# Output projection of two weight parts in one wide product, a second add per batch, and gaps in the order of work closed

## The chip, the cores and the metric

One core of one Trainium2 chip runs the whole program. The metric is the device time in microseconds (us), the median of several executions.

## The reference, cut to what matters

`x` is (32, 112, 256), `ctx_512` is (32, 375, 128), everything in float32.

```
x = x + tanh(g_xattn) * attention(layernorm(x), ctx, Wq, Wk, Wv, Wo, bo)     # 16 heads of 64
x = x + tanh(g_ffn)   * ffn(layernorm(x))
attention:  softmax(q k^T / 8) v, per head, then @ Wo + bo
ffn:        gates = softmax(xf @ router_w); top 2 of 14 experts, weights normalised
            sum of the 2 routed experts, plus 2 shared experts
            expert(x) = silu(rmsnorm(x) * rw @ W1) @ W2                      # 256 -> 512 -> 256
```

## The kernel before, in words

Every float32 product is made from two parts of each operand, `hi` (rounded to the fast matmul type) and `lo` (the rest): hi·hi, lo·hi and hi·lo are summed in PSUM. The function `three` (L584 to L588) issues these three matmuls, on the lines L586, L587 and L588.

**Attention** (`attend`). The weights are fused first: per head Wq Wk^T becomes `wqk`, and Wv Wo becomes `wvo` of 128 x 256, in the buffers `wvo_hi` and `wvo_lo`. Batches go in 16 pairs; of a pair, the 2 x 16 x 112 rows of scores make 28 steps of 128 rows. In a step, TensorE (PE) makes the scores of one tile (`scores`, 376 columns), a side job now and then (queries of two heads, the transposed context, the transposed x), the transposes of an earlier tile's probabilities (`turn`, L647), the weighted sums of the context (`sums`, 448 columns, a quad of four heads), and the output projection of single heads (`project`, 256 columns, into the left half of the bank `O`). VectorE (DVE) makes maxima (L872), reciprocals (L878), half of the scalings (L881) and all `lo` parts (L855); ScalarE (ACT) makes the exponentials (L763), the other scalings (L768) and all `hi` parts. GpSimd (POOL) splits the context, adds the bias, makes the Newton steps of the norms, and splits one routed expert's weights per pair (`split_expert`).

When the 16 heads of a batch are projected, DVE adds the bank `O` and the residual into `x2` (`ln2_add`, L911 to L916) and signals `x2_ready`. PE waits for `x2_ready` before the first head of the next batch (L671), because that head overwrites `O`. For the first batch of a pair the add falls into step 26; for the second it falls into step 12 of the next pair, just as the first projection of the next batch does.

PE, DVE and POOL run the first and the last pair as straight code, and pairs 1 to 14 in a hardware loop (`body_over_pairs`, L381; POOL L567); SP (the DMA issuer) loops over pairs 1 to 13 (L470); ACT is straight code.

**Start.** SP issues the loads in order: the two gates (L74, L75), x, Wk, Wq in two halves, and so on. PE first transposes Wk and Wq (L131, 24 transposes), then fuses.

**End of the attention.** In the last pair POOL makes `ln2_root(2p-1)`, `add_bias(p, 1)`, then scales the shared experts' weights (`scale_shared`, L1141) and splits them (`split_shared`, L1151). After the last step PE drains: it interleaves the first transposes of the normed rows (`sb["turn"]`, L1206) with the last sums and projections.

**Router, shared experts of groups 0 to 4** (`front`): 10 items of hidden (L1037, 512 columns) and output (L1045, 256 columns). The last item's output is preceded by the transposes of the first routed tile.

**Routed experts** (`routed_experts`): 69 tiles of 128 rows, each with hidden (L1702), transposes of the next rows (L1689), transposes of the hidden (L1712) and output: here `W2`'s hi and lo already lie side by side, so that output is one matmul of 512 columns (L1722) and one of 256 (L1726) per hidden block, and the two halves of the bank are added afterwards.

**Shared experts of groups 5 and 6** (`shared_after`), the sum, and the stores of `out` by SP (L1835), the last one of 512 KB.

## Time and profile before

| what | value |
|---|---|
| median of 3 runs | 1460.05 us (1459.97 to 1460.82) |
| the profiled execution's own time | 1458.97 us |
| its span, first to last instruction | 1457.2 us |
| mean granted TensorE clock | 0.999 |
| PE busy | 1435.2 us, 98% of the span, 9774 matmuls |
| PEld (weight loads, beside PE) | 1346.5 us, 92% |
| DVE busy | 1081.7 us, 74% |
| ACT busy | 935.1 us, 64% |
| POOL busy | 463.4 us, 32% |
| chain that ended last | PE 95%, DVE 2%, ACT 1%, issue 1% |

The busy share is an average over stages. A matmul's duration in the profile is its latency: the next one starts before it ends, so what a matmul costs is read from the distance of starts. "Idle before" names what ended the wait.

### The profile page before, as it was taken

What the parts mean: (1) busy time and instruction counts of PE and PEld (TensorE: products, weight loads), DVE (VectorE), ACT (ScalarE), POOL (GpSimd) and SP (SyncE); (2) the same over time, 40 slices, a digit from 0 to 9 for tenths busy, and PEclk for the clock granted to TensorE, in tenths of its full rate; (3) what the DMA queues carried; (4) which work ended last, traced back from release to release, by engine and by line L of the source; (5) the groups of instructions that cost most, each with busy time, mean ns of one, the idle gap of its engine ahead of it and who ended that gap; (6) DMA issues with size and microseconds to landing.
All of it is one profiled execution on the core that took longest, in us unless ns stands there. A gap on an engine that the chain in (4) does not pass through costs nothing.

```text
span 1457.2 us, 31992 instructions
## 1 busy us (share of the span) xinstructions
PE 1435.2 (98%) x9774; PEld 1346.5 (92%) x9774; DVE 1081.7 (74%) x2614; ACT 935.1 (64%) x2398; POOL 463.4 (32%) x688
## 2 busy tenths in 40 slices
PE   7999999999999999999999999999999999999998
PEld 7999999999999999999999999998789978888888
DVE  4878888888888888888788888878587444444448
ACT  6777777777776777777777777776453345455452
POOL 4313142231323413143231332417100145555520
PEclk9999999999999999999999999999999999999999
DMA  4010311213112131211303112150022346662235
GB/s 125 7 51 17 115 74 51 95 31 114 76 49 79 50 108 38 93 74 55 107 15 116 74 49 85 44 191 32 28 102 116 142 168 237 213 236 85 78 130 213
DMA packets 55583, 137.07 MB, mean 94 GB/s; under 512 B 10496, under 2 KB 38160, under 8 KB 51920
## 3 DMA queue, kind: packets, MB, share of 16 engines
q1 hardware_dynamic: 48880, 118.01, 23.4%
q0 software_dynamic: 6624, 18.13, 3.9%
q8 instruction: 35, 0.57, 0.2%
q14 instruction: 44, 0.36, 0.1%
HBM read 86.69 MB, written 49.43 MB: 93 GB/s over the span
## 4 chain that ended last, share of the span: by engine, by line
PE 95%; DVE 2%; ACT 1%; issue 1%; DMA 0%; SPq 0%; ACTq 0%; DVEq 0%
PE bank L586 19%; PE bank L587 18%; PE bank L588 18%; PE bank L647 10%; PE bank L1702 7%; PE bank L1045 6%; PE bank L1037 5%; PE bank L1722 4%; PE bank L1726 2%; PE bank L1712 2%; PE bank L1689 1%; PE bank L1218 1%; PE bank L602 1%; DVE pT_lo L855 1%; DVE nmax L872 0%
## 5 line engine op out<-in xcount | busy, mean ns | idle before, releaser
L763 ACT ACTIVATE prob<-bank,nmax 128x375 f32<-128x375 f32 x448 | 258.8, 578 | 190.3 <-DVE nmax L872 188.3
L855 DVE TENSOR_TENSOR pT_lo<-bank,pT_hi 125x384 fp32r<-125x384 f32 x448 | 246.2, 550 | 25.3 <-ACT pT_hi L774 23.7
L872 DVE TENSOR_REDUCE nmax<-bank 128x1 f32<-128x375 f32 x448 | 241.3, 539 | 29.9 <-PE bank L588 28.6
L647 PE MATMUL bank<-keep_ident,prob 128*125 128x128 f32 x1344 | 221.0, 273 | 0.9 <-DVE prob L881 0.9
L774 ACT CAST pT_hi<-bank 125x384 fp32r<-125x384 f32 x448 | 212.6, 475 | 1.7 <-PE bank L647 1.7
L647 PEld LDWEIGHTS bank<-keep_ident,prob 128*125 128x125 f32 x1344 | 201.4, 187 | 6.9 <-DVE prob L881 1.2
L586 PE MATMUL bank<-attend_wvo_hi,zT_hi 128*112 128x256 f32 x512 | 169.4, 331 | 0.7 <-DVE x L916 0.7
L586 PE MATMUL bank<-pT_hi,kv_hi 125*128 125x448 f32 x384 | 152.8, 398 | 4.3 <-DVE zT_lo L855 1.6
L586 PE MATMUL bank<-attend_kvT_hi,qp_hi 128*128 128x376 f32 x448 | 152.0, 339 | 1.4 <-ACT prob L763 1.3
L587 PE MATMUL bank<-attend_kvT_hi,qp_lo 128*128 128x376 f32 x448 | 149.8, 334 | 0.0
L588 PE MATMUL bank<-attend_kvT_lo,qp_hi 128*128 128x376 f32 x448 | 149.0, 333 | 0.0
L587 PE MATMUL bank<-attend_wvo_hi,zT_lo 128*112 128x256 f32 x512 | 144.2, 282 | 0.0
L855 DVE TENSOR_TENSOR qp_lo<-bank,qp_hi 128x448 fp32r<-128x448 f32 x128 | 79.7, 623 | 86.8 <-ACT qp_hi L756 85.0
L588 PE MATMUL bank<-attend_wvo_lo,zT_hi 128*112 128x256 f32 x512 | 143.7, 281 | 0.0
L518 POOL TENSOR_SCALAR rs<-mv 112x1 f32<-112x1 f32 x32 | 7.1, 221 | 422.7 <-DVE mv L925 422.6
L587 PE MATMUL bank<-xnT_hi,attend_wqk_lo 128*128 128x224 f32 x512 | 140.7, 275 | 0.0
L587 PE MATMUL bank<-pT_hi,kv_lo 125*128 125x448 f32 x384 | 140.7, 366 | 0.0
L588 PE MATMUL bank<-pT_lo,kv_hi 125*128 125x448 f32 x384 | 140.6, 366 | 0.0
L588 PE MATMUL bank<-xnT_lo,attend_wqk_hi 128*128 128x224 f32 x512 | 140.3, 274 | 0.0
L586 PE MATMUL bank<-xnT_hi,attend_wqk_hi 128*128 128x224 f32 x512 | 139.7, 273 | 0.6 <-DVE attend_wqk_lo L206 0.3
L768 ACT ACTIVATE prob<-prob,prob_inv 128x375 f32<-128x375 f32 x224 | 136.8, 611 | 1.4 <-DVE prob_inv L878 1.4
L881 DVE TENSOR_SCALAR prob<-prob,prob_inv 128x375 f32<-128x375 f32 x224 | 114.2, 510 | 8.0
(238 smaller groups left out, 3724.8 us busy)
## 6 DMA issues: line engine op xcount, KB each, us to landing
w_split<-we_split SPq DMA_DIRECT2D x14, 2048.0 KB, 6.9
keep_weights<-w_split SPq DMA_DIRECT2D x14, 2048.0 KB
we_in<-in_w SPq DMA_DIRECT2D x28, 512.0 KB, 5.9
keep_y_all<-y_rows SPq DMA_DIRECT2D x14, 512.0 KB, 9.1
kv_in<-in_ctx SPq DMA_DIRECT2D x32, 187.5 KB
h_rows<-hrow SPq DMA_DIRECT2D x32, 112.4 KB, 2.3
keep_h_in<-h_rows SPq DMA_DIRECT2D x7, 514.0 KB, 9.3
x_in<-in_x SPq DMA_DIRECT2D x16, 224.0 KB, 2.8
```

What stands on the lines that cost most here:

```text
L586: nc.tensor.matmul(out, a[0], b_[0], start=start, stop=False)
L587: nc.tensor.matmul(out, a[1], b_[0], start=False, stop=False)
L588: return nc.tensor.matmul(out, a[0], b_[1], start=False, stop=stop)
L647: last = nc.tensor.transpose(turn_bank_of(s)[0:MP, c * P:(c + 1) * P], prob[:, s % NB, c * MP:(c + 1) * MP], ident[:])
L763: nc.scalar.activation(prob[:, s % NB, :], score_bank(s)[:, 0:M], ACT.Exp, bias=nmax[:, s % NB:s % NB + 1], accum_out=psum_[:, s % NB:s % ...
L768: nc.scalar.mul(prob[:, s % NB, :], prob[:, s % NB, :], pinv[:, s % NB:s % NB + 1]).then_inc(norm_act, 1)
L774: nc.scalar.copy(pT["hi"][:, :, ring_place(s)], turn_bank_of(s)[0:MP, 0:MC * P].rearrange("p (c n) -> p c n", c=MC)).then_inc(pT_hi, 1)
L855: return nc.vector.tensor_tensor(dst, src, hi.bitcast(F32), ALU.subtract)
L872: nc.vector.tensor_reduce(nmax[:, s % NB:s % NB + 1], score_bank(s)[:, 0:M], AX, ALU.max, negate=True).then_inc(max_ready, 1)
L881: nc.vector.tensor_scalar(prob[:, s % NB, :], prob[:, s % NB, :], pinv[:, s % NB:s % NB + 1], None, ALU.mult).then_inc(norm_dve, 1)
L1045: last = nc.tensor.matmul(bank[:, (t % 2) * D:(t % 2 + 1) * D], hid[h][:, e, j, t * P:(t + 1) * P], sb["w2s_" + w][:, e, j, :], start=e == ...
L1702: last = nc.tensor.matmul(H_BANK[b][:, :], hT[a][:, b, k, :], part(slot, 2 * k * HID + at, HID), start=k == 0 and q == 0, stop=k == 1 and ...
```

## The change

- The two parts of the output weights lie side by side in one buffer `wvo` of [128, heads, 2, 256]; `wvo_hi` and `wvo_lo` become views of it. Per head, `project` issues one matmul of 512 columns (stationary zT_hi, moving hi and lo) and one of 256 columns (stationary zT_lo, moving hi) instead of three of 256. The hi·lo term then lies in the right half of `O`.
- `ln2_add` makes two adds, the second waits for the first, and `x2_ready` comes with the second.
- The loops over pairs of PE, DVE, POOL and SP are unrolled.
- The two gate loads are issued by ACT instead of SP. PE runs 20 transposes of the identity into an unused bank before it waits for Wk.
- POOL makes `scale_shared` ahead of `ln2_root(2p-1)` and of `add_bias(p, 1)`. `sb["turn"](pe, 1)` goes one step earlier in PE's drain.
- The first three tiles' rows are turned, and the first two routed hiddens made, between the parts of the last shared output. The routed stage's `T_BANK` and `O_BANK` are exchanged.
- The last store is cut into two of 256 KB.

```diff
-        def sync_gates(sp):
-            sp.dma_start(gates[:, 0:1], io["g_xattn"].partition_broadcast(P)).then_inc(gate_in, 16)
+        def sync_gates(act):
+            act.dma_start(gates[:, 0:1], io["g_xattn"].partition_broadcast(P)).then_inc(gate_in, 16)
...
+        def warm(pe):
+            pe.wait_ge(ident_ok, 1)
+            for _ in range(20):
+                nc.tensor.transpose(banks[7][:, 0:P], sb["ident"][:], sb["ident"][:])
...
         def body_over_pairs(eng, body):
-            body(0, FULL)
-            with eng.Fori(1, PAIRS - 1) as p:
-                body(p, FULL)
-            body(PAIRS - 1, LAST)
+            for p in range(PAIRS):
+                body(p, LAST if p == PAIRS - 1 else FULL)
...
             split_context(p, 1)
+            sb["scale_shared"](pool)
             ln2_root(2 * p - 1)
             add_bias(p, 1)
-            sb["scale_shared"](pool)
...
-                last = three(O[0:N, 0:D], [zT[q][:, qd % 2, j * N:(j + 1) * N] for q in ("hi", "lo")],
-                             [sb["wvo_" + q][:, h, :] for q in ("hi", "lo")], h == 0, h == H - 1)
+                hi, lo = (zT[q][:, qd % 2, j * N:(j + 1) * N] for q in ("hi", "lo"))
+                nc.tensor.matmul(O[0:N, :], hi, sb["wvo"][:, h, :, :].rearrange("p q d -> p (q d)"), start=h == 0,
+                                 stop=h == H - 1, skip_group_check=True)
+                last = nc.tensor.matmul(O[0:N, 0:D], lo, sb["wvo_hi"][:, h, :], start=False, stop=h == H - 1,
+                                        skip_group_check=True)
...
-            for s in range(last_tile(7) + 4, last_tile(7) + 6):
-                behind(last, s, (), True)
+            behind(last, last_tile(7) + 4, (), True)
             sb["turn"](pe, 1)
-            for s in range(last_tile(7) + 6, last_tile(7) + 9):
+            for s in range(last_tile(7) + 5, last_tile(7) + 9):
...
-                nc.vector.tensor_tensor(x2[:, b, :], O[0:N, 0:D], x_res[:, b, :], ALU.add).then_inc(x2_ready, 1)
+                nc.vector.tensor_tensor(x2[:, b, :], O[0:N, 0:D], x_res[:, b, :], ALU.add).then_inc(x2_half, 1)
+                dve.wait_ge(x2_half, bi + 1)
+                nc.vector.tensor_tensor(x2[:, b, :], O[0:N, D:2 * D], x2[:, b, :], ALU.add).then_inc(x2_ready, 1)
...
-               ("wvo_hi", [P, H, D], F32R), ("wvo_lo", [P, H, D], F32R)]
+               ("wvo", [P, H, 2, D], F32R)]
...
-            sb["turn_first_rows"](pe)
-            output(len(items) - 1)
+            sb["turn_rows"](pe, 0)
+            output(len(items) - 1, (0,))
+            sb["turn_rows"](pe, 1)
+            output(len(items) - 1, (1,))
+            sb["routed_hidden"](pe, 0)
+            output(len(items) - 1, (2,))
+            sb["routed_hidden"](pe, 1)
+            sb["turn_rows"](pe, 2)
+            output(len(items) - 1, (3,))
...
-            sb["split_first_rows"](dve)
-            for t in range(4):
-                accumulate(len(items) - 1, t)
+            sb["split_rows"](dve, 0)
+            sb["split_rows"](dve, 1)
+            for t in (0, 1):
+                accumulate(len(items) - 1, t)
+            sb["split_rows"](dve, 2)
+            for t in (2, 3):
+                accumulate(len(items) - 1, t)
...
-        HT_BANK, H_BANK, T_BANK, O_BANK = banks[0:2], banks[2:4], banks[4:6], banks[6:8]
+        HT_BANK, H_BANK, T_BANK, O_BANK = banks[0:2], banks[2:4], banks[6:8], banks[4:6]
...
+            g = GROUPS - 1
+            for t in (0, 2):
+                sp.wait_ge(acc_done, 4 * (g - BEFORE) + t + 2)
+                sp.dma_start(by_group(io["out"], g)[:, t:t + 2, :], acc[:, 4 * g + t:4 * g + t + 2, :]).then_inc(out_stored, 16)
```

## Rows read from the trace of the kernel before

**Rows 1.** The page's part 4: the chain that ended last.
```profile
PE 95%; DVE 2%; ACT 1%; issue 1%; DMA 0%; SPq 0%; ACTq 0%; DVEq 0%
```
**Rows 2.** Windows: stretch, us; then PE, PEld, DVE, ACT, POOL busy; clock, DMA.
```profile
500.00:560.00 60.00, 59.90 (x430) 58.19 (x429) 50.37 (x130) 43.84 (x122) 16.68 (x31) 1.00 0.22 74
```
**Rows 3.** Groups by line and form: the first matmul of each head's projection.
```profile
L586 PE MATMUL bank<-attend_wvo_hi,zT_hi 128*112 128x256 f32 x512 | 169.4, 331 | 0.7 <-DVE x L916 0.7
```
**Rows 4.** Timeline of PE (start, us, engine, line), projections after transposes and after other matmuls.
```profile
476.14 0.36 PE L586 MATMUL bank<-attend_wvo_hi,zT_hi 128*112 128x256 f32 x1
476.34 0.28 PE L587 MATMUL bank<-attend_wvo_hi,zT_lo 128*112 128x256 f32 x1
...
479.37 0.28 PE L586 MATMUL bank<-attend_wvo_hi,zT_hi 128*112 128x256 f32 x1
...
479.72 0.28 PE L586 MATMUL bank<-attend_wvo_hi,zT_hi 128*112 128x256 f32 x1
```
**Rows 5.** Chain in order of time: 48 matmuls of 256 columns, 24 of 512.
```profile
1058.28 5.76 PE bank L1045 x48
1064.04 5.47 PE bank L1037 x24
```
**Rows 6.** Timeline: adds and PE's next projection, steady loop and pair 15.
```profile
548.76 0.42 DVE L916 TENSOR_TENSOR x<-bank,x_res 112x256 f32<-112x256 f32 x1
...
549.32 0.36 PE L586 MATMUL bank<-attend_wvo_hi,zT_hi 128*112 128x256 f32 x1
...
1011.74 0.41 DVE L916 TENSOR_TENSOR x<-bank,x_res 112x256 f32<-112x256 f32 x1
...
1012.30 0.34 PE L586 MATMUL bank<-attend_wvo_hi,zT_hi 128*112 128x256 f32 x1 [0.67 <-DVE x L916]
```
**Rows 7.** Timeline: add of a first batch, and DVE's next idle time.
```profile
516.50 0.42 DVE L916 TENSOR_TENSOR x<-bank,x_res 112x256 f32<-112x256 f32 x1
...
518.95 0.62 DVE L855 TENSOR_TENSOR qp_lo<-bank,qp_hi 128x448 fp32r<-128x448 f32 x1 [1.05 <-ACT qp_hi L756]
```
**Rows 8.** Timeline: PE's weight load after its longest wait in a pair.
```profile
522.99 0.19 PEld L586 LDWEIGHTS bank<-pT_hi,kv_hi 125*128 125x128 f32 x1 [0.29 <-issue]
```
**Rows 9.** Timeline of the start, and a DMA row (KB, us to landing).
```profile
0.82 0.39 SPq L74 DMA_DIRECT2D gates<-in_g_xattn  x1
...
1.74 0.42 SPq L394 DMA_DIRECT2D x_in<-in_x  x1
...
6.54 1.94 PE L131 MATMUL bank<-keep_ident,under_wk 128*128 128x128 f32 x8 [6.54 <-DMA under_wk<-in_Wk]
...
8.27 3.24 PE L131 MATMUL bank<-keep_ident,under_wq 128*128 128x128 f32 x16
...
24.97 1.09 PE L131 MATMUL bank<-keep_ident,under_wv 128*128 128x128 f32 x8
...
under_wq<-in_Wq SPq DMA_DIRECT2D x2, 512.0 KB, 5.8
```
**Rows 10.** Timeline of the last pair's end: POOL, DVE and the waits of PE.
```profile
1013.67 2.38 POOL L1158 TENSOR_TENSOR keep_w1s_lo<-keep_w_in,keep_w1s_hi 128x1024 fp32r<-128x1024 f32 x1
...
1014.87 1.40 DVE L881 TENSOR_SCALAR prob<-prob,prob_inv 128x375 f32<-128x375 f32 x1
...
1016.32 0.59 PE L647 MATMUL bank<-keep_ident,prob 128*125 128x128 f32 x3 [0.94 <-DVE prob L881]
...
1023.20 0.44 PE L586 MATMUL bank<-pT_hi,kv_hi 125*128 125x448 f32 x1 [1.02 <-DVE zT_lo L855]
```
**Rows 11.** Timeline where the routed experts begin.
```profile
1164.44 0.76 DVE L1558 TENSOR_TENSOR keep_acc<-bank,keep_acc 128x256 f32<-128x256 f32 x2 [1.98 <-PE bank L1045]
...
1170.24 0.49 PE L1702 MATMUL bank<-keep_weights,keep_tile_hT_hi 128*128 x1 [1.34 <-DVE keep_tile_hT_lo L1788]
...
1173.46 0.49 PE L1702 MATMUL bank<-keep_weights,keep_tile_hT_hi 128*128 x1 [0.91 <-DVE keep_tile_hT_lo L1788]
```
**Rows 12.** DMA issues: the stores of the result.
```profile
out<-keep_acc SPq DMA_DIRECT2D x7, 512.0 KB, 2.6
```

More of the change, by code:

```diff
@@ L469, in sync @@
             body(0, FULL)
-            with sp.Fori(1, PAIRS - 2) as p:
+            for p in range(1, PAIRS - 2):
                 body(p, FULL)
@@ L566, in gpsimd @@
             body(0, True)
-            with pool.Fori(1, PAIRS - 1) as p:
+            for p in range(1, PAIRS - 1):
                 body(p, False)
@@ L694, in tensor @@
             Q0, Q1, Q2, Q3 = (Q[u] for u in range(4))
+            weights["warm"](pe)
             for i in range(6):
@@ L1249, in hidden, with output @@
                     shared_hidden(nc, sb, g, e, j, H_BANK[j]).then_inc(h_done, 1)
-            def output(i):
+            def output(i, parts=range(4)):
                 e = items[i][1]
                 pe.wait_ge(hid_lo_ok, 4 * i + 4)
-                for t in range(4):
+                for t in parts:
                     if e == 0 and items[i][0] > 0 and t % 2 == 0:
@@ L1609, in vector @@
                     decode()
-            sb["split_first_rows"](dve)
-            for t in range(4):
+            sb["split_rows"](dve, 0)
[4 more added lines that the diff above has]
+            for t in (2, 3):
                 accumulate(len(items) - 1, t)
@@ L1691, in turn_rows, with part, hidden @@
             last.then_inc(h_turned, 1)
-        def tensor(pe):
-            def part(slot, at, n):
-                return weights[:, bass.ds(slot, 1), at:at + n].rearrange("p s n -> p (s n)")
-            def hidden(t, slot):
-                b = t % 2
-                pe.wait_ge(hT_lo, t + 1)
-                for k in range(2):
-                    for q, (a, at) in enumerate((("hi", 0), ("lo", 0), ("hi", HID))):
-                        last = nc.tensor.matmul(H_BANK[b][:, :], hT[a][:, b, k, :], part(slot, 2 * k * HID + at, HID),
-                                                start=k == 0 and q == 0, stop=k == 1 and q == 2)
-                last.then_inc(hid_done, 1)
+        slots = {}
+        def part(slot, at, n):
+            return weights[:, bass.ds(slot, 1), at:at + n].rearrange("p s n -> p (s n)")
+        def hidden(pe, t):
+            b = t % 2
+            slot = slots[t] = pe.value_load(ring_of[0:1, t:t + 1], min_val=0, max_val=RING - 1)
+            pe.wait_ge(hT_lo, t + 1)
+            for k in range(2):
+                for q, (a, at) in enumerate((("hi", 0), ("lo", 0), ("hi", HID))):
+                    last = nc.tensor.matmul(H_BANK[b][:, :], hT[a][:, b, k, :], part(slot, 2 * k * HID + at, HID),
+                                            start=k == 0 and q == 0, stop=k == 1 and q == 2)
+            last.then_inc(hid_done, 1)
+        def tensor(pe):
             def turn_hidden(t):
@@ L2022, in build @@
                 sb.setdefault(n + "_at", nc.sbuf_base - 4 * int(np.prod(s[1:])))
+        sb["wvo_hi"], sb["wvo_lo"] = (sb["wvo"][:, :, i, :] for i in range(2))
         program(nc, io, sb, banks)
```

33 lines of the change are left out of this document (15 added, 18 removed).

## The prediction

> **What bounds the kernel now.** I read the chain that ended last first: 95% of it is PE [rows 1]. Then a window in the middle of the attention: PE is busy 59.90 of 60 us, DVE 50.37, ACT 43.84, POOL 16.68 [rows 2]. So PE sets the pace, DVE is the next engine, and a term counts only if it shortens PE's stream or lengthens a wait of PE. The groups by form give the count of what is changed, 512 heads [rows 3]. The timeline gives costs: durations there are latencies (the 0.28 us of a projection's matmul), so I take distances of starts. PE's longest wait in a pair of the loop is 0.29 us, seen at its weight loads [rows 8], so little of what PE loses in a pair can be made good by a later wait that shrinks.
>
> A measurement of this kernel can tell about 0.2% (2.9 us) from no change. The sum is made against the profiled execution, 1458.97 us, 1.1 us under the median of 1460.05; the differences are carried over to the median.
>
> **The projection.** Three matmuls of 256 columns take 479.72 - 479.37 = 0.35 us per head (0.354 by three times 0.118), and 48 of them elsewhere 5.76 us, 0.120 each; 24 of 512 columns take 5.47 us, 0.228 each [rows 4, 5]. After transposes the first one takes 0.20 instead of 0.12 [rows 4], an extra that I assume a wide one pays too. New: 0.228 + 0.119 = 0.347. With 0.354 before, 7 ns per head are saved: 512 x 7 ns = 3.6 us. Bounds: 0.360 before gives 13 ns or 6.7 us, 0.35 before gives 3 ns or 1.5 us. The columns are the same (768); what goes is one matmul's fixed part.
> The Trainium skill's page TensorE: Matmul & The Clock Gate, section "Wait — 56ns, not 53.3ns?", states that warm matmuls follow each other at columns over clock plus some 2.5 ns, which speaks against this edit: one matmul fewer per head would be worth 1.3 us in all, an estimate from that page. By that rule 256 columns take 0.109 us; the trace has 0.120 [rows 5], and the trace decides.
>
> **The second add.** It is like the first: 0.42 us [rows 6], plus some 0.03 us for the wait on its own engine, so `x2_ready` comes 0.45 us later. Who waits for it? For the second batch of a pair the add ends at 549.18 and PE's next projection starts at 549.32, 0.14 us later. In pair 15 PE truly waited (idle 0.67 us), and there the distance from the add's end, 1012.15, to the start, 1012.30, is the same 0.15 us [rows 6]. So the wait is already at its limit, with at most 0.02 us to spare, and the new 0.45 us goes almost wholly into PE's stream: 0.44 us. By the code the place comes once in each of the pairs 1 to 15, and the first batch of pair 15, which has waited already, makes 16: 16 x 0.44 = **+7.0 us**. Queued behind PE's waiting load are the rest of step 12 and all later steps. For the first batches of pairs 0 to 14 PE has a query job of 12 matmuls between the add and the next projection (the job of step 26), and waits for nothing; the delay of the maxima queued behind the add on DVE ends in DVE's idle time of 1.05 us [rows 7]. I cost those 15 at nothing; without that cover each costs up to 0.45 us. Bounds of the term: 0 (if DVE reaches its first add 0.45 us earlier) and 14 us. I take 7.0, by the nearest row.
>
> **The loops unrolled.** The window of [rows 2] is almost as long as a pair and holds a turn of PE's loop (it lies at the add of a first batch, step 26, and the step after it [rows 7]); PE is idle for 0.10 us in all of it. So a turn costs PE at most 0.10 us, 14 turns 1.4 us. Value 0, bounds -1.4 us and, with more instructions to load (a cost no row shows, bounded by the same number), +1.4. The same cover, queued matmuls, hides the turns of DVE, POOL and SP.
>
> **The start.** Without the two gate loads SP's other loads go out 1.74 - 0.82 = 0.92 us earlier, so PE's wait for Wk ends at 5.6 instead of 6.54. Both gates now stand in ACT's queue ahead of the tanh, which is early enough. The 24 transposes took 1.94 + 3.24 us, one in 0.21; the 8 at 24.97 took 1.09, one in 0.11 with overlap [rows 9]: twice the spacing, the 1.2 GHz level against the 2.4 GHz level, and before 6.54 PE had done nothing. The 20 warming transposes at 0.21 us are 4.3 us of work that can begin when the identity is made, within the first 2 us; they fill the wait, and PE should then be at the higher level, or get there in them. Wk and Wq's first half then take PE half the time, but Wq's second half, issued at about 3.2 and 5.8 us on its way [rows 9], comes at about 8.1 even when issued earlier; with 8 transposes behind it, PE is through at 9.0 to 10 instead of 11.5. I take -1.9 us (bounds -0.9, the loads alone, and -2.6). What follows is a chain over PE, ACT and DVE that shifts as a whole; POOL's splits are bound to later loads of SP and move by 0.92 us alone, and if they become late the gain is that, the first bound.
>
> **The end of the attention.** The `turn` moved ahead of the sums is 8 transposes, 0.87 us of starts by 0.11 each [rows 9], and fills as much of the wait of 1.02 [rows 10]: -0.9 us. POOL's `scale_shared`, six scalings, moves ahead of the five small instructions of a root and of one bias add, and with it the splits behind it. A long POOL instruction holds up DVE's scaling: L881 took 1.40 instead of 0.42 us until POOL's split of 2.38 us was done, and PE waited 0.94 [rows 10]. Earlier splits are over before the drain, where each such hold-up stands on PE's path; I take two of them with a follower, -2.5 us. The same instructions now meet DVE earlier in the pair, where queues are fuller: one more hold-up there, +1.0. Net -1.5 (bounds -3 and +1). Behind the moved step on POOL waits the root of the pair's first second norm, and ACT, in order, waits for that root: if POOL is late by a microsecond, so are the exponentials behind it; that is the upper bound.
>
> **The routed begin.** PE's waits of 1.34 and 0.91 us [rows 11] go. New: the first transposes of the hidden still wait for the four sums of the last shared item, and these now come right before: two adds of together 0.76 us [rows 11] and the handovers make 1.05 us. Net -1.2 us (bounds -2.25 and 0).
>
> **The tail.** The last store takes 2.6 us alone [rows 12], but queues behind two of the same size; half of it earlier gives 0 (bounds -0.9, +0.1).
>
> **Sum:** -3.6 + 7.0 + 0 - 1.9 - 0.9 - 1.5 - 1.2 + 0 = **-2.1 us**: 1456.9 in the profiled execution's terms, 1458.0 in the median's.
>
> **Rivals.**
> - *The second add stays hidden.* If DVE comes to its first add earlier, since PE, held up once, no longer runs ahead, the +7.0 goes or halves: 1451.0, or 1454.5. Against it stands the equal distance of 0.15 us in both cases of [rows 6]. 0.20.
> - *DVE sets the pace* (slower). At one place, step 26, the second add pushes the maxima and the lo parts behind it; if the idle 1.05 us [rows 7] is needed by ACT's chain, PE's wait of 0.29 us [rows 8] grows by the full 0.45 in 15 pairs: +6.8, 1464.7. It decides if more than the idle time is used up between the add and the wait. DVE is busy 50.4 of 60 us [rows 2], which speaks against. 0.12.
> - *The gaps are not filled*: POOL's collisions merely move, the routed begin gets a new wait as long as the old ones, PE isn't at its upper clock in time. Then only 0.9 of the start is left: -3.6 + 7.0 - 0.9 = +2.5, 1462.5. 0.08.
> - *The merge saves little*: the fixed part per matmul is small, and the lower bound of the rows, 1.5 us instead of 3.6, holds. The sum is 0.0: 1460.1. 0.05.
>   This is the case of the Trainium skill's page TensorE: Matmul & The Clock Gate, section "Wait — 56ns, not 53.3ns?"; so far the trace speaks against it.
>
> That the change doesn't do what it says is possible only for the clock and the gaps, which are in the third.
>
> **How the numbers follow.** Forecast, 0.55: 1458.0, its own range 1455.5 to 1460.5; a third of that case (0.18) lies over 0.2% below the median, 0.35 within, 0.02 above. With rival 1 faster is 0.38; rivals 3 and 4 give 0.10 to within and 0.03 to slower; with rival 2 slower is 0.17, within 0.45. Range: 1453.0 takes in half of rival 1, 1463.5 takes in rivals 3 and 4 and leaves out rival 2; 0.2 stays outside.
>
> **What would show it.** After: a head's projection in 0.347 us; in each pair a wait of PE for `x` of L916's second add, of 0.3 to 0.45 us, at one place, so a period of about 62.3 us against 62.1; PE's first transposes of Wk at 0.11 us; no DVE L881 above 1 us after the last maxima; at the routed begin one wait of about 1 us for the sums. I'd be wrong if PE shows no wait for the add (then faster), or if it waits longer for the lo parts in step 0 (then slower).

## The result, and the profile after

The changed kernel takes 1470.82 us (median of 4 runs, 1470.08 to 1471.36) against 1460.01 us: the ratio is 1.0075, 95% interval 1.0062 to 1.0088. It is slower by 0.75%, 10.8 us. The prediction was 1458.0 (1453.0 to 1463.5).

The page of the changed kernel (span, busy time and instructions by engine, TensorE's clock by slices, shares of the chain, two groups):

```profile
span 1469.6 us, 28533 instructions
PE 1438.5 (98%) x9282; PEld 1318.4 (90%) x9282; DVE 1105.4 (75%) x2646; ACT 934.5 (64%) x2398; POOL 458.4 (31%) x688
PEclk9999999999999999999999999998999999999999
PE 80%; DVE 12%; ACT 5%; issue 3%; DMA 0%; ACTq 0%; POOL 0%; POOLq 0%
L675 PE MATMUL bank<-attend_wvo,zT_hi 128*112 128x512 f32 x512 | 224.5, 445 | 3.2 <-DVE x L923 3.2
L587 PE MATMUL bank<-pT_hi,kv_hi 125*128 125x448 f32 x384 | 152.7, 398 | 15.4 <-DVE zT_lo L860 12.4
```

Three things differ from the page before. PE's share of the chain fell from 95% [rows 1] to 80%, DVE's rose from 2% to 12%. The group of the projection has the wait for the second add, 3.2 us in all. And the group of the context matmuls has a wait of 12.4 us for `zT_lo`, of which nothing was predicted.

The timeline (start, duration, engine, line, operation, tiles; in brackets the idle time ahead and who ended it), at the start, in a steady pair, and in the last pair:

```profile
1.59 4.19 PE L123 MATMUL bank<-keep_ident 128*128 128x128 f32 x20 [1.59 <-POOL keep_ident L91]
6.83 1.09 PE L135 MATMUL bank<-keep_ident,under_wk 128*128 128x128 f32 x8 [1.05 <-DMA under_wk<-in_Wk]
...
10.30 1.09 PE L135 MATMUL bank<-keep_ident,under_wq 128*128 128x128 f32 x8 [0.88 <-DMA under_wq<-in_Wq]
...
549.58 0.41 DVE L921 TENSOR_TENSOR x<-bank,x_res 112x256 f32<-112x256 f32 x1
550.03 0.42 DVE L923 TENSOR_TENSOR x<-bank,x 112x256 f32<-112x256 f32 x1
...
550.60 0.46 PE L675 MATMUL bank<-attend_wvo,zT_hi 128*112 128x512 f32 x1 [0.21 <-DVE x L923]
...
995.21 0.74 POOL L494 TENSOR_TENSOR x_res<-x_res,attend_bo 112x256 f32<-112x256 f32 x1
...
995.89 1.04 POOL L1162 CAST keep_w1s_hi<-keep_w_in 128x1024 fp32r<-128x1024 f32 x1
...
996.87 1.04 POOL L1162 CAST keep_w2s_hi<-keep_w_in 128x1024 fp32r<-128x1024 f32 x1
996.92 12.37 DVE L886 TENSOR_SCALAR prob<-prob,prob_inv 128x375 f32<-128x375 f32 x1
997.87 2.34 POOL L1165 TENSOR_TENSOR keep_w1s_lo<-keep_w_in,keep_w1s_hi 128x1024 fp32r<-128x1024 f32 x1
...
1006.73 2.35 POOL L1165 TENSOR_TENSOR keep_w2s_lo<-keep_w_in,keep_w2s_hi 128x1024 fp32r<-128x1024 f32 x1
...
1009.97 0.71 PE L587 MATMUL bank<-pT_hi,kv_hi 125*128 125x448 f32 x1 [12.06 <-DVE zT_lo L860]
```

One norm, L886, whose median is 0.42 us, takes 12.37. It begins 0.05 us after GpSimd's second CAST and ends at 1009.29, 0.2 us after the last of GpSimd's eight instructions. `zT_lo` stands behind it on VectorE, and PE waits 12.06 us for `zT_lo`. The windows of that stretch (stretch, length, then PE, PEld, DVE, ACT, POOL busy, clock, DMA) show what follows:

```profile
990.00:1001.99 11.99, 6.98 (x41) 6.04 (x40) 10.58 (x17) 5.76 (x17) 9.93 (x13) 1.00 0.00 1
1001.99:1015.64 13.65, 5.67 (x18) 5.19 (x19) 10.70 (x11) 2.68 (x7) 7.09 (x5) 0.50 0.06 17
1015.64:1028.00 12.36, 12.34 (x75) 11.33 (x74) 10.09 (x26) 8.37 (x23) 0.00 (x0) 1.00 0.01 1
```

The granted clock falls to 0.50, the 1.2 GHz level, while PE stands still, and is back at 1.00 at 1015.64, when PE has been at work again since 1009.97. By milestones, before and after: first score matmul 25.82 and 25.94 us, first of the last pair 955.40 and 957.40, last score 1012.72 and 1028.31, first matmul of the shared experts 1044.2 and 1057.9, last matmul 1452.4 and 1464.7. So 2.0 us are lost up to the last pair, 11.7 in and behind it, and 1.3 won back at the routed experts. That is the account of the two profiled executions, which lie 12.4 us apart; the medians lie 10.8 apart.

### The profile page after: what moved, and what is told of

The parts are those of the page before. It is cut to its first block, busy times and chain, and to the rows that moved or that the text cites. A ratio compares the mean times of both kernels' runs of the same rounds, so it can differ in the third digit from the quotient of the medians.

```text
span 1469.6 us, 28533 instructions
## 1 busy us (share of the span) xinstructions
PE 1438.5 (98%) x9282; PEld 1318.4 (90%) x9282; DVE 1105.4 (75%) x2646; ACT 934.5 (64%) x2398; POOL 458.4 (31%) x688
## 4 chain that ended last, share of the span: by engine, by line
PE 80%; DVE 12%; ACT 5%; issue 3%; DMA 0%; ACTq 0%; POOL 0%; POOLq 0%
PE bank L587 12%; PE bank L588 11%; PE bank L589 11%; PE bank L648 7%; PE bank L1722 7%; PE bank L675 6%; PE bank L1052 5%; PE bank L1044 5%; PE bank L1743 4%; PE bank L677 3%; DVE pT_lo L860 3%; DVE nmax L877 2%; PE bank L1747 2%; PE bank L1733 2%; ACT prob L767 2%
## 5 line engine op out<-in xcount | busy, mean ns | idle before, releaser
L860 DVE TENSOR_TENSOR pT_lo<-bank,pT_hi 125x384 fp32r<-125x384 f32 x448 | 245.7, 549 | 27.4 <-ACT pT_hi L778 25.9
L675 PE MATMUL bank<-attend_wvo,zT_hi 128*112 128x512 f32 x512 | 224.5, 445 | 3.2 <-DVE x L923 3.2
L587 PE MATMUL bank<-pT_hi,kv_hi 125*128 125x448 f32 x384 | 152.7, 398 | 15.4 <-DVE zT_lo L860 12.4
L677 PE MATMUL bank<-attend_wvo,zT_lo 128*112 128x256 f32 x512 | 143.3, 280 | 0.0
L886 DVE TENSOR_SCALAR prob<-prob,prob_inv 128x375 f32<-128x375 f32 x224 | 134.4, 600 | 8.0
L860 DVE TENSOR_TENSOR qp_lo<-bank,qp_hi 128x448 fp32r<-128x448 f32 x128 | 79.5, 621 | 78.7 <-ACT qp_hi L760 78.6
L1808 DVE TENSOR_TENSOR keep_tile_hT_lo<-bank,keep_tile_hT_hi 128x256 fp32r<-128x256 f32 x69 | 29.3, 424 | 110.3 <-ACT keep_tile_hT_hi L1768 110.3
```

The lines of the kernel that those rows point to most:

```text
L587: nc.tensor.matmul(out, a[0], b_[0], start=start, stop=False)
L675: nc.tensor.matmul(O[0:N, :], hi, sb["wvo"][:, h, :, :].rearrange("p q d -> p (q d)"), start=h == 0, stop=h == H - 1, skip_group_check=True)
L677: last = nc.tensor.matmul(O[0:N, 0:D], lo, sb["wvo_hi"][:, h, :], start=False, stop=h == H - 1, skip_group_check=True)
L860: return nc.vector.tensor_tensor(dst, src, hi.bitcast(F32), ALU.subtract)
L886: nc.vector.tensor_scalar(prob[:, s % NB, :], prob[:, s % NB, :], pinv[:, s % NB:s % NB + 1], None, ALU.mult).then_inc(norm_dve, 1)
```

## The experiments

Below, the period is the distance from the first score matmul of a pair to that of the next, in the middle of the loop: 62.10 us before, 62.20 to 62.24 after (two pairs 62.33 and 62.51). Kernels are timed beside the kernel before, and the ratio is that of the two.

**The parts one by one.** e1 is the kernel after with this undone:

```diff
-            sb["scale_shared"](pool)
             ln2_root(2 * p - 1)
             add_bias(p, 1)
+            sb["scale_shared"](pool)
```

> The kernel after, with scale_shared alone back behind add_bias, where the kernel before has it. Theory A (the place of split_shared decides: after the move it begins 8.9 us earlier and meets VectorE's scaling of prob, L886, which takes 12.37 us): no VectorE instruction of more than 3 us in the last pair, no PE wait of 12 us, TensorE's clock at full speed there, and 1458 to 1461 us, 10 to 12 us less than the kernel after. Rival B (the second add or the unrolling shifts VectorE's work under split_shared, wherever it stands): the long instruction stays, 1468 to 1472 us.

Measured: 1459.52 us, ratio 0.9993 (0.9984 to 1.0003). Theory A. The longest norm under `split_shared` is 1.55 us. e2 is the reverse edit in the kernel before:

> The kernel before, with scale_shared alone moved ahead of ln2_root and add_bias, as in the kernel after. Theory A (the move by itself causes the loss): split_shared begins at 995 to 997 us, one VectorE instruction is held up for 10 us or more, 1469 to 1472 us. Rival B (it is a coincidence of phase: what VectorE begins in the first 0.1 us of a GpSimd instruction is held, and the other edits set that phase): a hold-up of 1.5 us at most, as the three in the kernel before, and 1458 to 1461 us.

Measured: 1471.54 us, ratio 1.0077 (1.0052 to 1.0101), theory A, though `split_shared` begins at 994.14, a little earlier than expected. The move alone costs 11.4 us. The timeline has the same picture, with the norm 0.08 us behind the second CAST:

```profile
993.46 0.74 POOL L493 TENSOR_TENSOR x_res<-x_res,attend_bo 112x256 f32<-112x256 f32 x1
994.14 1.04 POOL L1155 CAST keep_w1s_hi<-keep_w_in 128x1024 fp32r<-128x1024 f32 x1
...
995.12 1.05 POOL L1155 CAST keep_w2s_hi<-keep_w_in 128x1024 fp32r<-128x1024 f32 x1
...
995.21 12.35 DVE L881 TENSOR_SCALAR prob<-prob,prob_inv 128x375 f32<-128x375 f32 x1
```

e3 is the kernel before with the merged projection and both adds, e11 the same with the second add left out:

```diff
-                nc.vector.tensor_tensor(x2[:, b, :], O[0:N, 0:D], x_res[:, b, :], ALU.add).then_inc(x2_half, 1)
-                dve.wait_ge(x2_half, bi + 1)
-                nc.vector.tensor_tensor(x2[:, b, :], O[0:N, D:2 * D], x2[:, b, :], ALU.add).then_inc(x2_ready, 1)
+                nc.vector.tensor_tensor(x2[:, b, :], O[0:N, 0:D], x_res[:, b, :], ALU.add).then_inc(x2_ready, 1)
```

> The kernel before, with the merged projection and its second add alone. Theory A (the two nearly cancel: the periods of the pairs rose by 0.10 to 0.14 us in the kernel after, 2.0 us over 14 pairs): 1461 to 1463 us, PE waiting 15 to 16 times for the second add with about 0.35 us of PE idle time a pair. Rival B (the second add costs its full 0.44 us 16 times and the merge saves 3.6 us, as predicted): 1463.4 us. Rival C (the rise of the periods comes from the unrolling): 1460 us or less.

> The kernel before with the merged projection but one add: the half of columns 256 to 511 (hi of the context by lo of the weights) is computed and left out of x2. Theory A (the merge by itself saves 0.23 us a pair in matmul time, part of it lost to small new stalls, and the second add costs 0.44 us a pair): 1456.5 to 1459 us, periods 61.9 to 62.06 us. Rival B (the merge saves nothing, what the matmuls give the following transposes take): 1460 us or more.

Measured: e3 1465.36 us (ratio 1.0033, 1.0023 to 1.0042), period 62.50; e11 1457.79 us (0.9981, 0.9970 to 0.9991), period 61.98, theory A of e11. So the merge saves 2.3 us and the second add costs 1465.36 - 1457.79 = 7.6 us. All three theories of e3 were too low: in the kernel after, something else had to be paying for the adds. It is the unrolling, e4, the three loops of the kernel before written out as in the change:

> The kernel before with its three loops over the pairs unrolled, nothing else. Theory A (instruction loading is hidden): 1459 to 1461 us, periods of the pairs 62.10 us as before, although the packets of instruction loading double. Rival B (loading or the missing branch shows): periods above 62.2 us or below 62.0, the time off by more than 1.4 us.

Measured: 1455.62 us, ratio 0.9969 (0.9958 to 0.9980), period 61.83. Rival B: 4.5 us faster. One place where it gains can be seen in the timeline, the score matmul of step 22. Before:

```profile
568.22 0.28 PE L588 MATMUL bank<-attend_wvo_lo,zT_hi 128*112 128x256 f32 x1
568.42 0.43 PE L586 MATMUL bank<-attend_kvT_hi,qp_hi 128*128 128x376 f32 x1
568.69 0.33 PE L587 MATMUL bank<-attend_kvT_hi,qp_lo 128*128 128x376 f32 x1
```

And e4, the same instructions, and the weight load that answers to [rows 8]:

```profile
520.99 0.19 PEld L584 LDWEIGHTS bank<-pT_hi,kv_hi 125*128 125x128 f32 x1 [0.21 <-DVE pT_lo L853]
...
566.16 0.28 PE L586 MATMUL bank<-attend_wvo_lo,zT_hi 128*112 128x256 f32 x1
566.28 0.39 PE L584 MATMUL bank<-attend_kvT_hi,qp_hi 128*128 128x376 f32 x1
566.51 0.33 PE L585 MATMUL bank<-attend_kvT_hi,qp_lo 128*128 128x376 f32 x1
```

The distances are 0.20 and 0.27 us before, 0.12 and 0.23 in e4, and in neither is there an idle bracket: matmuls overlap, so PE counts as busy while it loses 0.12 us. The weight load of [rows 8] waited 0.29 us for "issue", in e4 it waits 0.21 us for `pT_lo` itself.
```diff
+            if eng is nc.tensor:
+                for p in range(1, PAIRS - 1):
+                    body(p, FULL)
+            else:
                 with eng.Fori(1, PAIRS - 1) as p:
```

> The kernel before, with the loop over the pairs unrolled on TensorE alone; VectorE, GpSimd and SyncE keep their loops. Theory A (the 4.5 us of the unrolling come from TensorE's queue, where a register operation stands beside most waits and delays the matmul behind them): periods of 61.83 us, 1455 to 1456.5 us. Rival B (they come from VectorE's queue, which hands data over earlier): periods of 62.10 us, 1459 to 1461 us.

Measured: 1458.28 us (0.9985, 0.9974 to 0.9997), period 62.02. Neither theory: TensorE's queue gives 0.08 us of a pair's 0.27, most of it at the wait of [rows 8]; the other 0.19 come only when the other loops go too, most of it at the score matmul of step 22. Before and in e7 alike that matmul starts 1.20 us after the end of VectorE's low part of the query (`qp_lo`), while in e4, where that part stands 0.17 us further ahead of the projection in front of the matmul, it follows the projection at once. So the 0.12 us that PE loses there are not due to its own queue; that the loop of VectorE, which makes the low part, is the cause is likely, but the other three loops were not tried one by one.

e8 is the kernel after without merge, second add and the moved scaling; e12 takes the edits of the start out of e8 too:

> The kernel after without the merged projection and second add and with scale_shared back at its old place: unrolled, start, drain, routed begin and tail as changed. Theory (the parts add up: before 1460.0, unrolling -4.5, routed begin -1.3, start and drain -0.2 to -1.0): 1453 to 1454.5 us, faster than both kernels. Rival (the gain of the unrolling comes back elsewhere, or start and drain cost): 1455 us or more.

> The kernel of e8 without the edits of the start: the gates' transfers back on SyncE's queue, no 20 warming transposes. Theory A (the start gains nothing: the first transpose of Wk waits for its DMA in either form): 1454.0 to 1455.2 us, the same as e8 within 0.6. Rival B (the predicted 1.9 us are there): 1456 us or more. Rival C (the start costs: first fused matmul at 11.4 us without, 11.2 to 12.9 with): 1453 to 1454 us.

Measured: e8 1454.65 us (0.9958, 0.9945 to 0.9971), e12 1454.25 us (0.9954, 0.9937 to 0.9972). **Both beat both kernels; the one before, measured beside them, by 5.1 and 5.8 us.** e8 lies 0.15 us above the range of its theory. The start brings nothing, theory A of e12; over all kernels here the first score matmul starts between 25.6 and 27.2 us, with and without the edit.

**Why one norm took 12.37 us.** That the move causes it left open how: other norms that meet a GpSimd instruction are held until that one has ended [rows 10], not until eight have. First the phase. e5 is the kernel after with a small GpSimd copy ahead of the block:

```diff
+            nc.gpsimd.tensor_copy(sb["w1s_hi"][:, 0, 0, 0:256], w1_in[:, 0, 0, 0:256]).then_inc(late_ok, 1)
+            pool.wait_ge(late_ok, 1)
             sb["split_shared"](pool, 0)
```

> The kernel after, with one further GpSimd copy (128x256, 0.2 to 0.4 us) ahead of split_shared, so that its eight instructions begin that much later; everything else stands where it does in the kernel after. Theory A (a coincidence of 0.1 us: VectorE's L886 begins at the moment at which GpSimd passes from its first CAST to its second, and then stays locked out until the last of the eight has ended): the 12.37 us instruction is gone, hold-ups of 0.5 to 2.6 us are left, each ended by the end of a GpSimd instruction; 1458.5 to 1461 us. Rival B (work of VectorE that meets split_shared at this stage is locked out until it ends, whatever the phase): still one instruction of 10 to 13 us, 1469 to 1472 us. Rival C (other norms fall on the next handover): another length, 3 to 9 us, and 1462 to 1468 us.

Measured: 1460.82 us, the longest hold-up 2.55 us, and a norm that begins where L886 did takes 0.69. That spoke for theory A, a coincidence of 0.1 us. I tested it with a probe behind the end of the kernel, on the two engines alone:

```diff
+        for r in range(60):   # GpSimd
+            pool.wait_ge(go, r + 1)
+            CAST, CAST, subtract, subtract, CAST, CAST, subtract, subtract   # 128x1024 each
+        for r in range(60):   # VectorE
+            reduce 64 columns -> go; reduce n(r) columns; scale 128x375
```

> The kernel before, whole, and behind its end a probe that only VectorE and GpSimd run, 60 times: GpSimd runs CAST, CAST, subtract, subtract twice on 128x1024 (14 us), VectorE one scaling of 128x375, which begins 17 ns later each time, over 1.0 us, so that it meets each phase of the first CAST and the handover to the second. Theory A (handover): most scalings are held until the CAST in progress ends (0.4 to 1.5 us long), and 2 to 8 of the 60, that begin in the first 0.1 us of the second CAST, take 10 us or more. Rival B (it takes more than these two engines, or another cause): none is above 3 us. Time of the whole: 850 to 900 us more than the kernel before.

> The probe of e6 behind the end of the kernel before, finer (4 ns a step, 60 steps from 40 ns ahead of the second CAST to 200 ns into it), with TensorE transposing and ScalarE copying bank to SBUF beside it, and with the reciprocal ahead of the scaling that takes its result, as in the attention. Theory A (the other engines' traffic or the reciprocal is what e6 lacked): 5 to 20 of the 60 scalings take 10 us or more. Rival B (the hold-up needs something else of the attention): all are held until the CAST in progress ends, 1.0 to 1.3 us.

Measured: none of the 120 scalings took more than 1.30 us. Those of e6 that began 0, 19, 36, 51, 68 and 85 ns into the second CAST took 1.25 to 1.16 us, and all ended 0.21 us after that CAST. Rival B both times. In place I fared no better. e9 and e14, with their edits of `split_expert`:

```diff
+                for v in (1024, 538 + 22 * e, 256):   # e9, ahead of the CASTs
+                    nc.gpsimd.tensor_copy(we[:, at:at + v], we_in[:, 0:v]).then_inc(shift, 1)
+                m = 510 - 6 * e                       # e14
+                nc.gpsimd.tensor_copy(dst[:, :, 0, 0:m], src[:, :, 0:m]).then_inc(we_step, 1)
+                nc.gpsimd.tensor_copy(dst2[:, :, 0, :], src2).then_inc(we_step, 1)
+                nc.gpsimd.tensor_copy(dst[:, :, 0, m:HID], src[:, :, m:HID]).then_inc(we_step, 1)
```

> The unrolled kernel before, with three further GpSimd copies (128x1024, 128x538 to 128x824, 128x256) ahead of the two CASTs of split_expert in pairs 1 to 14, the middle one 22 elements wider in each pair: so the second CAST begins 18 ns later from pair to pair, over 0.24 us about the moment at which VectorE begins the norm that lies 44.13 us into the pair. Theory A (a norm that begins 0.03 to 0.1 us into a GpSimd CAST, with the attention running, is locked out of every handover until GpSimd's queue is empty): in 2 to 6 of the 14 pairs that norm takes 5 to 8 us, in the others 1.0 to 1.3 us. Rival B (the moment alone isn't enough): none above 2 us. The time itself says nothing: 1456 to 1500 us.

> The unrolled kernel before; split_expert of each pair leaves its scaling by rms_e out (the routed outputs are not scaled) and begins with its CASTs: the first CAST 1020 elements wide in pair 1 and 12 fewer in each later pair, the rest of its columns cast after the second CAST. So the second CAST begins from 0 to 0.15 us ahead of the norm that lies 38.57 us into the pair, one step of 10 ns a pair, with the attention running as in the stretch of the loss. Theory A (the moment, within the attention, decides): in 2 to 8 of 14 pairs that norm takes 5 us or more. Rival B (the moment alone does not, here as in the probes): all 14 take 1.0 to 1.3 us.

In e9 the copies widened from pair to pair, but VectorE's instructions were held along with them and the norm began 0.70 us into the CAST in all 14 pairs: the scan did not scan, and says nothing. In e14 norms that began 53 to 182 ns into the second CAST, with the attention running, took 1.20 to 1.07 us. Rival B. The theory of the moment had all but fallen. Two edits of the kernel after ran beside it, e13 with pauses, e15 with a shorter first CAST:

```diff
                 pool.wait_ge(w_step, 3 * SHARED + 2 * e + n + 1)
+                need(pool, w_lo, 2 * e + n)                                       # e13
...
+                    nc.gpsimd.tensor_copy(hi[:, 0, :, 0:452], whole[:, 0, :, 0:452])   # e15, first CAST
+            nc.gpsimd.tensor_copy(hi[:, 0, :, 452:HID], whole[:, 0, :, 452:HID])       # e15, third CAST
+            pool.wait_ge(late_ok, 1)
```

> The kernel after; in split_shared the second subtract of an expert now waits for the first to have ended, and the subtract of the second expert for those of the first, so that GpSimd's queue has pauses of about 0.1 us, the first behind the first subtract. All ahead of that stands at the same time as in the kernel after, the norm's begin too. Theory A (the norm stays locked out only as long as GpSimd's instructions follow each other without a pause): it ends at the first pause, 3.3 to 3.7 us long instead of 12.37, and the kernel takes 1460 to 1463 us. Rival B (once locked out it waits for the whole block, pauses or not): 12 us or more, 1470 us or more.

> The kernel after; the first CAST of split_shared is cut to 904 of its 1024 elements a partition, and the rest is cast behind the second CAST. So the second CAST begins 0.10 us earlier, 0.15 us ahead of the norm instead of 0.05. Theory A (only the first 0.1 us of a CAST locks a norm out for long): the norm is held until the CAST has ended, 1.0 to 1.2 us, and the kernel takes 1459 to 1462 us. Rival B (every norm that begins in the second CAST is locked out here): 12 us or more, 1470 us or more.

```profile
994.87 0.73 POOL L494 TENSOR_TENSOR x_res<-x_res,attend_bo 112x256 f32<-112x256 f32 x1
...
997.53 2.34 POOL L1166 TENSOR_TENSOR keep_w1s_lo<-keep_w_in,keep_w1s_hi 128x1024 fp32r<-128x1024 f32 x1
...
1000.01 2.37 POOL L1166 TENSOR_TENSOR keep_w2s_lo<-keep_w_in,keep_w2s_hi 128x1024 fp32r<-128x1024 f32 x1
...
996.59 3.50 DVE L886 TENSOR_SCALAR prob<-prob,prob_inv 128x375 f32<-128x375 f32 x1
```

e13 (these rows): the norm begins 0.06 us into the second CAST as before, passes the first handover locked out, and gets in at the first pause, 0.2 us after the first subtract's end: 3.50 us long; 1461.86 us, ratio 1.0016 (1.0006 to 1.0025). Theory A of e13. e15: the norm begins 0.15 us into the second CAST and takes 1.11 us; 1460.49 us (1.0009, 1.0000 to 1.0019). That is theory A of e15, the theory of the moment, and what follows leaves this one run unexplained.

What the probes lacked was the instructions ahead. e16 is e10 with a GpSimd add of 112x256 ahead of the eight, and a VectorE subtract ahead of the reciprocal:

```diff
+            nc.gpsimd.tensor_tensor(y[0:112], y[0:112], z[0:112], ALU.add)     # GpSimd, ahead of the eight
+            nc.vector.tensor_tensor(low, banks[0][:, 0:375], data, ALU.subtract)   # VectorE, ahead of the reciprocal
```

> The probe of e10 with VectorE's and GpSimd's instructions in the order and the spacing of the stretch of the loss: GpSimd adds 112x256 and then runs the eight of split_shared back to back; VectorE runs a maximum, the subtract into SBUF, the reciprocal, the scaling. 60 steps of 3 ns from the beginning of the second CAST on. Theory A (the subtract or the add ahead is what the probes lacked): some scalings of 10 us or more. Rival B (it needs more than the order of instructions on the four engines): all held until the CAST ends, 1.0 to 1.3 us.

Its groups, and under them that of e10 for the same scaling:

```profile
L2005 DVE TENSOR_SCALAR keep_y_all<-keep_y_all 128x375 f32<-128x375 f32 x60 | 741.4, 12356 | 2.1
L1985 POOL TENSOR_TENSOR keep_y_all<-keep_y_all 112x256 f32<-112x256 f32 x59 | 42.8, 725 | 36.5 <-DVE keep_y_all L1999 36.5
```

```profile
L2000 DVE TENSOR_SCALAR keep_y_all<-keep_y_all 128x375 f32<-128x375 f32 x59 | 61.6, 1044 | 2.1
```

Sixty of sixty scalings take 12.3 to 12.5 us, whatever their moment. Then two kernels with twelve cases each, five repetitions a case; e18 also has one edit in the kernel after itself:

```diff
+            pool.wait_ge(res_ready, B)
             pool.wait_ge(side_done, job_index(p, Q[7]) + 1)
             sb["split_shared"](pool, 0)
```

> The probe of e16, in which all 60 scalings took 12.3 to 12.5 us, in twelve cases of five repetitions (8 elements, 8 ns, apart). 0: as e16, the scaling 0.06 us into the second CAST. 1: no GpSimd add ahead. 2: add ahead, VectorE's subtract replaced by a maximum. 3: add ahead, then a pause before the first CAST. 4: a CAST of 128x256 in the add's place. 5: add ahead, four CASTs and then four subtracts. 6: the scaling 0.5 us into the second CAST. 7: in the middle of the first CAST. 8: in the first subtract. 9: no add, in the first subtract. 10: no add, no VectorE subtract (the probe of e10). 11: as 4, without VectorE's subtract. Theory A (GpSimd instructions that follow each other without a pause from before the scaling's request keep VectorE out; the instruction ahead of the two CASTs makes the difference): 0, 2, 4, 5, 6, 7, 8, 11 take 8 us or more, 1, 3, 9, 10 less than 3 us. Rival B (VectorE's own subtract ahead makes it): 0, 1, 3, 4, 5, 6, 7, 8, 9 long, 2, 10, 11 short. Rival C (both are needed): 2, 10, 11 and 1, 3, 9 short.

> The kernel after with one edit, GpSimd waits for its own add_bias to have ended before split_shared begins (a pause of about 0.1 us, no instruction moved), and behind its end twelve further cases of the probe, five repetitions each. In the kernel itself, Theory A (the add of 112x256, with the block behind it without a pause, is what locks VectorE out, as in cases 0 to 8 of e17): L886 is held 1.5 us at most, the last score matmul stands at 1013 to 1018 us instead of 1028.3; Rival B: 12 us again, 1028 us. In the cases, with the scaling 0.06 us into the second CAST, or nearby: Theory A1 (an add on fewer than 128 partitions does it): long (over 8 us) for adds of 112 and 64 partitions, in place or not, short for the add of 128; Theory A2 (any add or subtract ahead): long for 128 too, and for the subtract of 128x1024. A copy of 112x256 ahead: long only if the partitions alone decide (A3). A first CAST in two rows of 452: short, as in e15. Scalings between the add and the CASTs: short, as in the kernel before. A pause behind the first CAST: short. The request during the add itself: long. A subtract from SBUF in the scaling's place: long, if VectorE is kept out as a whole.

Measured in e17: long, 10.8 to 12.9 us, in cases 0, 2, 5, 6, 7, 8; short, 1.1 to 2.0 us, in 1, 3, 4, 9, 10, 11, each ended 0.21 us after the GpSimd instruction in progress. So VectorE's subtract (2) and the moment (6, 7, 8) don't matter, a pause behind the add (3) or no add (1, 9, 10) makes it short, and so does a copy of 128x256 in the add's place (4, 11). Theory A but for 4 and 11. Cases 0 and 4 of e17:

```profile
1468.69 0.73 POOL L1987 TENSOR_TENSOR keep_y_all<-keep_y_all 112x256 f32<-112x256 f32 x1 [0.62 <-DVE keep_y_all L2012]
1469.36 2.02 POOL L1998 CAST keep_weights<-keep_silu 128x1024 fp32r<-128x1024 f32 x2
...
1470.41 12.36 DVE L2028 TENSOR_SCALAR keep_y_all<-keep_y_all 128x375 f32<-128x375 f32 x1
...
1753.35 0.40 POOL L1991 COPY keep_y_all<-keep_y_all 128x256 f32<-128x256 f32 x1 [0.32 <-DVE keep_y_all L2012]
...
1754.75 1.18 DVE L2028 TENSOR_SCALAR keep_y_all<-keep_y_all 128x375 f32<-128x375 f32 x1
```

Measured in e18: long, 12.3 to 13.6 us, with an add on 112 partitions ahead (in place or not), an add on 64, **a copy on 112**, a scaling on 112, a first CAST in two rows, the request during the add itself, and a subtract from SBUF in the scaling's place; short, 0.8 to 1.2 us, with an **add on 128**, a subtract on 128, a pause behind the first CAST; and with two scalings of 128x512 between the add and the CASTs the request, 1.44 to 1.48 us into the first of them, was not held (0.42 to 0.46 us). Add on 128, copy on 112, and the edited kernel itself:

```profile
1541.86 0.73 POOL L2013 TENSOR_TENSOR keep_y_all<-keep_y_all 128x256 f32<-128x256 f32 x1 [0.34 <-DVE keep_y_all L2054]
1543.57 1.18 DVE L2073 TENSOR_SCALAR keep_y_all<-keep_y_all 128x375 f32<-128x375 f32 x1
...
1685.67 0.40 POOL L2017 COPY keep_y_all<-keep_y_all 112x256 f32<-112x256 f32 x1 [0.60 <-DVE keep_y_all L2054]
1687.07 12.36 DVE L2073 TENSOR_SCALAR keep_y_all<-keep_y_all 128x375 f32<-128x375 f32 x1
...
995.01 0.74 POOL L494 TENSOR_TENSOR x_res<-x_res,attend_bo 112x256 f32<-112x256 f32 x1
995.82 1.04 POOL L1163 CAST keep_w1s_hi<-keep_w_in 128x1024 fp32r<-128x1024 f32 x1
...
996.72 0.42 DVE L887 TENSOR_SCALAR prob<-prob,prob_inv 128x375 f32<-128x375 f32 x1
```

In the probes of e16 to e18 that decides: **a GpSimd instruction on fewer than 128 partitions (112 and 64 were tried), with the block of CASTs and subtracts on 128x1024 behind it without a pause, keeps VectorE out at every handover until GpSimd's queue first pauses.** There its operation (add, copy, scaling) doesn't matter, and VectorE's moment doesn't either.

In the kernel after, the add of `add_bias` (112 partitions) stands directly ahead of `split_shared`. In the kernel before, two things stood between them: the six scalings of `scale_shared`, and behind them a pause, since `split_shared` waits until the last scaling has ended (1004.64 to 1004.77):

```profile
1001.79 2.85 POOL L1149 TENSOR_SCALAR keep_w_in<-keep_w_in,keep_tanh_g 128x1024 f32<-128x1024 f32 x1
1004.77 1.04 POOL L1155 CAST keep_w1s_hi<-keep_w_in 128x1024 fp32r<-128x1024 f32 x1
```

A pause by itself is enough: with one of 0.07 us put there in the kernel after (e18), and nothing moved, the last score matmul stands at 1017.4 us instead of 1028.3, and the shared experts begin 10.9 us earlier. e5 fits as well, since its copy (128 partitions) has such a pause behind it.

Three places don't fit or are left open. In e15 the add on 112 partitions is followed by the CASTs without a pause, and the norm got in after 1.11 us. The case of e18 meant as its model was long, but it isn't the same: there the rest of the cut CAST runs ahead of the second CAST and the scaling's request falls into it, in e15 it runs behind. Whether the scalings alone, without the pause, would have protected the kernel before is open: in the case of e18 with scalings the request fell into a scaling and not into the CASTs. And in the attention's steady pairs a norm begins 0.08 us into an instruction on 112 partitions (112x2) that has a CAST of 125x384 behind it without a pause. Where GpSimd's loop is unrolled it takes 0.77 us and ends 0.21 us after that CAST (13 pairs of the kernel after, 14 of e4); where GpSimd loops (before, e3, e7, 14 pairs each) it takes 0.42 us at the same moment to within 10 ns, and it is the CAST that takes 0.71 us instead of 0.51. So what stands in GpSimd's queue between two instructions can matter where their records show no pause. Why was not tried.

## Why the prediction was wrong

| term | predicted, us | measured, us | from |
|---|---|---|---|
| merged projection | -3.6 (-6.7 to -1.5) | -2.3 | e11 |
| second add | +7.0 | +7.6 | e3 less e11 |
| unrolling | 0 (-1.4 to +1.4) | -4.5 | e4 |
| start | -1.9 (-2.6 to -0.9) | +0.4, nothing | e8 less e12 |
| `turn(1)` earlier | -0.9 | -0.9 | last score to logits, 14.69 in e4, 13.81 in e12 |
| GpSimd's order | -1.5 (-3 to +1) | +11.4; +11.3 | e2; after less e1 |
| routed begin | -1.2 | -1.3 | shared begin to fourth routed tile, 132.8 before, 131.5 after |
| tail | 0 | 0 | last matmul to end, 4.89 before, 4.92 after |

The column measured sums to +10.3 us (with +0.4 for the start and +11.3 for GpSimd's order), the change to +10.8. The parts don't add up exactly: those of e8 sum to -6.3 us, and e8 gains 5.1.

**The step that failed is GpSimd's order:** the prediction put the earlier `scale_shared` and `split_shared` at -1.5 us, and they cost 11.4. It took the hold-ups of [rows 10], each ended by the end of one GpSimd instruction, as the form that a meeting of the two engines has, counted two that would be saved and "one more hold-up there, +1.0", and closed the upper side at +1.0 ("if POOL is late by a microsecond, so are the exponentials behind it"). What came was one norm kept out for 12.37 us through six handovers, and PE waiting 12.06 us behind it. Which instruction would stand directly ahead of the block after the move was in the diff and was not asked. No row of the kernel before shows a lock-out over several instructions, so the size could not be read; but nothing in the rows bounded it at one microsecond either, and the moved block would run 13 us while the attention's queues were full.

The saving was wrong too. With the lock-out gone but the move kept, PE takes 89.34 us (e18) and 89.99 us (e5) from the first score matmul of the last pair to the shared experts, and 88.31 us with the old order (e1). The drain gets shorter (12.73 us from the last score to the logits in e18, 13.31 in e1), but in the last pair PE waits 1.5 us for an exponential, a wait that e1 doesn't have. So the move costs about 1 us even then.

**The unrolling failed too**, in its bound: "PE is idle for 0.10 us in all of it. So a turn costs PE at most 0.10 us". The idle time of an engine whose instructions overlap doesn't bound what it loses, and the cost lay not at the turn (59.7 us into PE's pair) but at waits 2.3, 33.3 and 47.7 us into it. For a part of it the row was there: "issue" as the releaser of a wait of 0.29 us [rows 8] means that PE waited for its own queue.
The Trainium skill's page Runtime: NRT & Kernel Launch, section "Instruction fetch mechanics", has kernels prefer full unrolling because a taken branch can stall the fetch; the direction agrees with e4, the place doesn't, since the gain lay at the waits and not at the turn.

**The start failed** because the loads' issue was taken for what bounds them. They do go out 0.93 us earlier, and the clock's level was right: 8 transposes in 1.09 us instead of 1.94 [rows 9]. But Wk's first transpose begins at 6.83 us in the profile after, and at 6.5 to 7.0 in every kernel here with or without the edit: the transfer lands when it lands, and PE, twice as fast, waits for Wq instead.

**What held.** The second add cost what its 0.15 us of distance [rows 6] said, once in a pair: 0.52 us of period between e11 and e3, against 0.44. The merge's term had the right mechanism and was mis-sized. By distances of starts (means over the loop), a head that stands behind another matmul takes 0.349 us in e11 instead of 0.358, about as predicted; but 5 of 8 heads stand behind transposes, and there it takes 0.437 instead of 0.440. Weighted, that is 5 ns a head, an estimate of 2.6 us in all, where 3.6 were predicted and 2.3 measured. Drain and routed begin came within 0.1 us, the latter by the predicted mechanism: the waits of 1.34 and 0.91 us [rows 11] are gone, and one of 0.9 us for the sums has come. Of the rivals, none had the mechanism that decided. "The gaps are not filled" foresaw that GpSimd's collisions would save nothing, but not their size, kept 0.9 us of a start that brought nothing, and was wrong on the routed begin and on the clock.

## What to carry to other kernels

When GpSimd's instructions are reordered, look at which one ends up directly ahead of a long block on 128 partitions: if it works on fewer partitions, put a wait for its own end behind it, which cost 0.07 us in e18. A loop whose waits compare with register values can cost at tight waits, not only on the queue of the engine that sets the pace, and idle time doesn't show it: compare distances of starts, or take "issue" as a releaser at its word. And an edit that is argued from collisions of two engines should be timed alone first; here the three parts worth having (unrolling, drain, routed begin) were hidden under two that cost and one, the start, that did nothing.

## What was not expected of the hardware

- A VectorE scaling of 0.42 us was kept out for 12.4 us, through six handovers between GpSimd instructions, reproducibly (all 60 in e16). The Trainium skill's page SBUF — State Buffer, section "Who interferes with whom", says that the loser of the shared port pair waits for the whole instruction of the other; the scalings of e6 and e10 that were held agree (each ended 0.21 us after the instruction in progress), e16 does not.
- In the same stretch a subtract with one operand in PSUM, L860 at 996.27 us under the first CAST, took its 0.55 us undisturbed, while one with both operands in SBUF was locked out as the scaling was (12.5 us, e18).
- Unrolling took 2002 register operations off the queues of TensorE and VectorE and shortened the period by 0.27 us, although PE counts as busy for 59.90 of 60 us with the loops [rows 2] and 59.97 without.
